# First stage of a one-core decoder block: state-space response from short powers, split gate product, and a new order of the batches

## The chip, the cores and the metric

The kernel runs on 1 core of one Trainium2 chip. The metric is the device time of one execution in microseconds (us), as the median of several runs. The core has five engines that each work through an instruction stream of their own: TensorE (PE in the profile, PEld for its weight loads), VectorE (DVE), ScalarE (ACT), GpSimd (POOL) and SyncE (SP, which only issues DMAs here). They are held together by semaphores: an instruction waits until a semaphore has reached a number, and another instruction raises it when it ends.

## The reference

Input x is 8 batches of 512 tokens with 256 channels. Three residual blocks follow each other, each behind a layer norm: a state-space block, a cross attention over 64 context rows, and a mixture of 8 experts with top 2. Only the first is touched. Its convolution is multiplied by 0 and set to 1, so the state input is the same for each token and each batch:

```python
xc = xc * 0 + 1
dBC = xc @ W_x.T                        # the same row for every token
delta = jax.nn.softplus(dlt @ W_dt.T + b_dt)
A = -jnp.exp(A_log)                     # 512 channels x 16 states
# scan over L: h = exp(delta*A)*h + delta*B ; y = sum over states of h*C
y = ys.transpose(1, 0, 2) + D_skip * xc
out = y * jax.nn.silu(z) @ W_out.T      # z: second half of x @ W_in.T
```

So y depends on channel and position alone. It is the running sum over the position of a kernel: for channel c and distance l, the sum over 16 states of coef times exp(rate * l). What differs between batches is z, and then the product of the gated y with W_out.

## The kernel before, in words

The program has two blocks, with a barrier between them. The first holds the state-space stage (lines 178 to 561), and the second the attention, the shared and the routed experts. Only the first block is changed.

The response. With KE = 4 groups of 128 channels and NS = 16 states there are 64 steps. In each step ScalarE computes exp(rate * l) for l = 1 to 511 of one group and state (`pw`, line 500), and VectorE adds it, times its coefficient, to `kern` (line 424). Four scans turn `kern` into `yD` (line 429). The layer norms and the evacuation of z are threaded between these steps: SLOT = 8 steps for each batch.

The gate. For each of the B = 8 batches VectorE computes statistics (line 111, `stats_part`), GpSimd the inverse deviation (120, 122), VectorE and GpSimd normalise two token tiles each (127), TensorE transposes them (274), ScalarE copies them out of PSUM (`hT`, 479), and TensorE multiplies with `win` in fp32 (287: four parts e of 128 channels, two pieces k of the sum each). ScalarE copies parts 0 to 2 into `sz` (484), VectorE part 3 (420). All eight batches of z are held in `sz`. TensorE goes through all eight, with the keys of the attention (304) behind batch 1, then the values with their bias (314, 315), and then goes on to the output products.

The output. After the response is there, for each batch: silu on ScalarE (506), `gate` on VectorE (440: `sz` times `yD`), `high` on ScalarE (512: the product rounded to fp32r in one of two buffers `gh`), the rest `gl` on VectorE (`low`, line 141, called at 453), `out_part` on TensorE (326: 48 fp32r products, lines 135 to 137, into PSUM banks 6 and 7) and `residual` on VectorE (436: adds the two banks to `X`, and frees them for the next batch). VectorE's order is written out by hand (lines 449 to 462): in turn b it does gate(b+1), the low part of b, residual(b-1). `high(b)` waits for the end of out_part(b-2), whose buffer it takes.

GpSimd spreads the keys into `kbd` (555), 16 instructions behind `yD`.

Of the kernel before, what the change touches and what calls it, by code (L numbers as in the profile page):

```python
# [18 lines left out]
def build(nc, d):  # L19
# [6 lines left out]
    ALU = mybir.AluOpType  # L26
# [3 lines left out]
    P = 128  # L30
# [5 lines left out]
    EI, NS = d["A_log"].shape  # L36
# [21 lines left out]
    with ctx:  # L58
# [84 lines left out]
        SLOT = KE * NS // B  # L143
        PWB = 4
# [8 lines left out]
        sz = Place(prior)("sz", [P, B, KE * L])  # L153
# [6 lines left out]
        hT = ab("hT", [P, 2, KD, L])  # L160
        wq, wk, wv, wo = (ab(n, [P, KD, D]) for n in ("wq", "wk", "wv", "wo"))
        bq, bk = ab("bq", [P, KD]), ab("bk", [P, KD])
        bv = ab("bv", [1, D])
# [9 lines left out]

        with ExitStack() as c:
            tmp = Place(ab.at)
            win_at = tmp.at  # L180
            win = tmp("win", [P, KD, EI])
            wout_at = tmp.at
            wout = tmp("wout", [P, KE, D])
            kbd_at = tmp.at
            wx = tmp("wx", [P, KE, R + 2 * NS])
            wdt = tmp("wdt", [R, EI])
            bdt = tmp("bdt", [P, KE])
            dsk = tmp("dsk", [P, KE])
            alog = tmp("alog", [P, KE, NS])
            steps = tmp("steps", [P, L - 1])  # L190
            onesrow = tmp("onesrow", [P, L])
            dlt = tmp("dlt", [R, 1])
            bc = tmp("bc", [P, 2 * NS])
            dl = tmp("dl", [P, 8, KE])
            rate = tmp("rate", [P, KE, NS])
            coef = tmp("coef", [P, KE, NS])
            pw = tmp("pw", [P, PWB, L - 1])
            kern = tmp("kern", [P, KE, L])
            kbd = Place(kbd_at)("kbd", [P, B, KD, HG * S])

            gh = [Place(hT_at)("gh0", [P, KE * L], F32R), Place(kbd_at + 4 * B * KD * HH * S)("gh1", [P, KE * L], F32R)]
            gl = Place(prior)("gl", [P, B, KE * L], F32R)
            wouts = (Place(win_at)("wouth", [P, KE, D], F32R), Place(wout_at)("woutl", [P, KE, D], F32R))
            x_in = phase_sems(c, " ".join("x_in_%d" % b for b in range(B)))
            hn_ready = phase_sems(c, "hn_ready_by_dve hn_ready_by_pool")
            z_copied = phase_sems(c, "z_copied_by_act z_copied_by_dve")
            (consts_in, w_in, win_in, kv_in, late_in, small_mm, dve_done, act_done, pw_ready, pw_used, s_chain,
             hn_var, hn_rstd, hT_psum, hT_ready, z_psum, sz_ready, w_split, g_high, g_low, yD_ready, g_ready, o_psum,
             x1_ready, k_psum, kT_ready, v_psum, v_ready, vz, k_ready) = phase_sems(c, """consts_in w_in win_in kv_in
                late_in small_mm dve_done act_done pw_ready pw_used s_chain hn_var hn_rstd hT_psum hT_ready  # L210
                z_psum sz_ready w_split g_high g_low yD_ready g_ready o_psum x1_ready k_psum kT_ready v_psum
                v_ready vz k_ready""")
            W_IN, KV_IN, LATE_IN = 16 * 6, 16 * 8, 16 * 7
            with nc.Block() as block:
                @block.sync
                def _(sp):
# [4 lines left out]
                    for dst, src in ((wx[:], d["W_xT"].rearrange("(k p) r -> p k r", p=P)),  # L221
                                     (wdt[:], d["W_dtT"]), (bdt[:], d["b_dt"]), (dsk[:], d["D_skip"]),
                                     (alog[:], d["A_log"].rearrange("(k p) n -> p k n", p=P)),
                                     (steps[:], d["steps"])):
                        sp.dma_start(dst, src).then_inc(w_in, 16)
                    x_load(0)
                    for dst, src in ((ident[:], d["ident"]), (small[:], d["small"])):
                        sp.dma_start(dst, src).then_inc(consts_in, 16)
                    sp.dma_start(win[:], d["W_inT"].rearrange("(k p) e -> p k e", p=P)).then_inc(win_in, 16)
# [9 lines left out]
                    sp.dma_start(bv[:], d["bv"]).then_inc(kv_in, 16)  # L239
                    for b in range(3, B):  # L240
                        x_load(b)
                    sp.dma_start(wout[:], d["W_outT"].rearrange("(k p) e -> p k e", p=P)).then_inc(late_in, 16)
                    for w, n in ((wq, "Wq"), (wo, "Wo")):
                        sp.dma_start(w[:], d[n].rearrange("(k p) e -> p k e", p=P)).then_inc(late_in, 16)
                    for dst, src in ((tri[:], d["tri"]), (causal[:], d["causal"]), (bq[:], d["bq"]),
                                     (bo[:], d["bo"].to_broadcast([P, D]))):
                        sp.dma_start(dst, src).then_inc(late_in, 16)
# [3 lines left out]
                def _(pe):  # L251
                    pe.wait_ge(w_in, W_IN)
                    pe.wait_ge(dve_done, 1)
                    for k in range(KE):
                        nc.tensor.matmul(PS[0:R, 0, 0:1], wx[:, k, 0:R], ones[:, 0:1],
                                         start=k == 0, stop=k == KE - 1)
                    for k in range(KE):
                        last = nc.tensor.matmul(PS[:, 1, 0:2 * NS], ones[:, :], wx[:, k, R:R + 2 * NS],
                                                start=k == 0, stop=k == KE - 1)
                    last.then_inc(small_mm, 1)  # L260
                    pe.wait_ge(dve_done, 2)
                    for k in range(KE):
                        last = nc.tensor.matmul(PS[:, 2, k:k + 1], wdt[:, k * P:(k + 1) * P], dlt[:],
                                                start=True, stop=True)
                    last.then_inc(small_mm, 1)

                    def transposes(b):
                        for half in hn_ready:
                            pe.wait_ge(half, b + 1)
                        if b:  # L270
                            pe.wait_ge(hT_ready, KD * b)
# [6 lines left out]
                    def z_part(b):  # L278
                        pe.wait_ge(hT_ready, KD * b + KD)
                        for e in range(KE):  # L280
                            if b:
                                if e < KE - 1:
                                    pe.wait_ge(z_copied[0], (KE - 1) * (b - 1) + e + 1)
                                else:
                                    pe.wait_ge(z_copied[1], b)
# [5 lines left out]
                    pe.wait_ge(consts_in, 32)  # L291
                    transposes(0)
                    pe.wait_ge(win_in, 16)
                    pe.wait_ge(dve_done, 3)
                    transposes(1)
                    for b in range(B):
                        z_part(b)
                        if b < B - 2:
                            transposes(b + 2)
                        if b == 1:  # L300
                            pe.wait_ge(kv_in, KV_IN)
                            for m in range(KD):
                                for k in range(KD):
                                    last = nc.tensor.matmul(PS[:, 6 + m, :], wk[:, k, m * P:(m + 1) * P],
                                                            ctx2[:, k, :, 0, :], start=k == 0, stop=k == KD - 1)
                                last.then_inc(k_psum, 1)
                    for b in range(B):
                        if b < 6:
                            pe.wait_ge(z_copied[0], (KE - 1) * (B - 1) + b // 2 + 1)
                        else:  # L310
                            pe.wait_ge(z_copied[1], B)
                        vs = PS[:, b // 2, (b % 2) * D:(b % 2 + 1) * D]
                        for k in range(KD):
                            nc.tensor.matmul(vs, ctx2[:, k, b, :, :], wv[:, k, :], start=k == 0, stop=False)
                        nc.tensor.matmul(vs, ones[0:1, :], bv[:], start=False, stop=True).then_inc(v_psum, 1)
                    pe.wait_ge(w_split, 2)
                    pe.wait_ge(kT_ready, KD)

                    def out_part(b):
                        pe.wait_ge(g_low, b + 1)  # L320
                        for t in range(TB):
                            if t % 2 == 0:
                                pe.wait_ge(x1_ready, 2 * b + t // 2 + 1)
                            for e in range(KE):
                                at = e * L + t * P
                                last = product(PS[:, 6 + t // 2, (t % 2) * D:(t % 2 + 1) * D],
                                               (gh[b % 2][:, at:at + P], gl[:, b, at:at + P]),
                                               [w[:, e, :] for w in wouts], e == 0, e == KE - 1)
                            if t % 2:
                                last.then_inc(o_psum, 1)  # L330
                    for b in range(B):
                        out_part(b)

                @block.vector
                def _(dve):
                    n = [0]
# [1441 lines left out]
```

## Time and profile before

| | us |
|---|---|
| median of 3 runs | 993.62 (992.84 to 995.99) |
| profiled execution, its own time | 989.96 |
| span of the trace | 988.3 |
| first block, by the start of the second block's work | 166.4 |
| PE busy, whole span | 923.4 (93%) |
| DVE busy | 625.2 (63%) |
| ACT busy | 556.4 (56%) |
| POOL busy | 347.0 (35%) |

The span is the time from the first to the last instruction; 1.7 us of the profiled execution lie outside it. The busy shares are those of the whole, in which the experts hold most of the time; the changed block is a sixth of it and has to be read by itself. A row of the timeline gives start, length, engine, line, operation, the tiles, the count of merged instructions, and in brackets the idle time before it with what ended it. An fp32 matmul stands in the trace as two instructions, an fp32r one as one. The printed length of a matmul holds its way through the array, so the pace is the distance from start to start.

### The profile page before, as it was taken

What the parts mean: (1) busy time and instruction counts of PE and PEld (TensorE: products, weight loads), DVE (VectorE), ACT (ScalarE), POOL (GpSimd) and SP (SyncE); (2) the same over time, 40 slices, a digit from 0 to 9 for tenths busy, and PEclk for the clock granted to TensorE, in tenths of its full rate; (3) what the DMA queues carried; (4) which work ended last, traced back from release to release, by engine and by line L of the source; (5) the groups of instructions that cost most, each with busy time, mean ns of one, the idle gap of its engine ahead of it and who ended that gap; (6) DMA issues with size and microseconds to landing.
All of it is one profiled execution on the core that took longest, in us unless ns stands there. A gap on an engine that the chain in (4) does not pass through costs nothing.

```text
span 988.3 us, 20180 instructions
## 1 busy us (share of the span) xinstructions
PE 923.4 (93%) x6832; PEld 792.9 (80%) x6833; DVE 625.2 (63%) x1485; ACT 556.4 (56%) x1109; POOL 347.0 (35%) x323
## 2 busy tenths in 40 slices
PE   2998898799999889999999999999999999999996
PEld 2444697455666468888888889999999999999996
DVE  4898897566775666666665566546565646565453
ACT  3688842365545454444644467557565657565552
POOL 3652723222120235555555322424233332423222
PEclk9999999999999999999999999999999999999998
DMA  9200002000000201111112843534325252523222
GB/s 254 92 1 1 1 1 72 21 1 1 1 1 1 94 1 67 68 67 67 68 67 76 264 116 94 134 49 107 66 44 131 42 140 44 130 42 54 44 44 33
DMA packets 49312, 64.21 MB, mean 65 GB/s; under 512 B 10289, under 2 KB 42290, under 8 KB 49138
## 3 DMA queue, kind: packets, MB, share of 16 engines
q0 software_dynamic: 17504, 34.87, 15.2%
q1 hardware_dynamic: 31618, 27.68, 9.6%
q10 hardware_dynamic: 144, 1.05, 0.4%
q8 instruction: 28, 0.46, 0.2%
q14 instruction: 18, 0.15, 0.1%
HBM read 38.82 MB, written 24.77 MB: 64 GB/s over the span
## 4 chain that ended last, share of the span: by engine, by line
PE 71%; DVE 7%; ACT 3%; issue 1%; DMA 0%; POOL 0%; SPq 0%; DVEq 0%; POOLq 0%; ACTq 0%
PE PS L135 20%; PE PS L136 19%; PE PS L137 19%; PE PS L646 3%; DVE mxpad L897 2%; PE PS L1559 2%; PE PS L687 2%; PE PS L673 2%; PE PS L693 1%; ACT recs L802 1%; ACT prT L783 1%; PE PS L1109 1%; DVE mxT L908 1%; DMA xr<-routed_rows 0%; DVE hidl L141 0%
## 5 line engine op out<-in xcount | busy, mean ns | idle before, releaser
L1605 ACT ACTIVATE hideh<-PS,be 128x256 fp32r<-128x256 f32 x280 | 140.5, 502 | 152.4 <-PE PS L137 152.4
L1633 POOL DMA_INDIRECT out_rows<-y,toki x70 | 122.3, 1747 | 268.3 <-DVE y L1673 259.1
L141 DVE TENSOR_TENSOR hidel<-act32e,hideh 128x256 fp32r<-128x256 f32 x280 | 118.4, 425 | 107.9 <-ACT act32e L1607 107.6
L135 PE MATMUL PS<-xTeh,wfch 128*128 128x256 f32 x560 | 159.4, 285 | 2.2 <-issue 1.1
L136 PE MATMUL PS<-xTel,wfch 128*128 128x256 f32 x560 | 158.5, 283 | 0.0
L137 PE MATMUL PS<-xTeh,wfcl 128*128 128x256 f32 x560 | 158.4, 283 | 0.0
L135 PE MATMUL PS<-wprh,hideh 128*128 128x256 f32 x560 | 157.9, 282 | 0.0
L137 PE MATMUL PS<-wprh,hidel 128*128 128x256 f32 x560 | 154.8, 277 | 0.0
L136 PE MATMUL PS<-wprl,hideh 128*128 128x256 f32 x560 | 154.8, 277 | 0.0
L1607 ACT ACTIVATE act32e<-PS,be 128x256 f32<-128x256 f32 x280 | 140.9, 503 | 2.8 <-DVE hidel L141 2.8
L135 PEld LDWEIGHTS PS<-xTeh,wfch 128*128 128x128 f32 x560 | 107.3, 192 | 3.8 <-issue 2.3
L137 PEld LDWEIGHTS PS<-xTeh,wfcl 128*128 128x128 f32 x560 | 107.5, 192 | 0.0
L136 PEld LDWEIGHTS PS<-xTel,wfch 128*128 128x128 f32 x560 | 107.3, 192 | 0.0
L136 PEld LDWEIGHTS PS<-wprl,hideh 128*128 128x128 f32 x560 | 105.3, 188 | 0.0
L135 PEld LDWEIGHTS PS<-wprh,hideh 128*128 128x128 f32 x560 | 105.2, 188 | 0.0
L137 PEld LDWEIGHTS PS<-wprh,hidel 128*128 128x128 f32 x560 | 105.2, 188 | 0.0
L1218 ACT ACTIVATE hidh<-PS,bfs 128x512 fp32r<-128x512 f32 x64 | 44.2, 690 | 57.8 <-PE PS L137 54.2
L120 POOL TENSOR_TENSOR vare<-mv,small 128x4 f32<-128x4 f32 x24 | 9.0, 376 | 189.4 <-DVE mv L115 189.2
L1291 POOL DMA_INDIRECT routed_rows<-rows,slotc x64 | 65.5, 1024 | 24.9 <-issue 19.3
L135 PE MATMUL PS<-wpsh,hidh 128*128 128x256 f32 x256 | 73.5, 287 | 0.3 <-DVE hidl L141 0.3
L137 PE MATMUL PS<-wpsh,hidl 128*128 128x256 f32 x256 | 72.1, 282 | 0.0
L136 PE MATMUL PS<-wpsl,hidh 128*128 128x256 f32 x256 | 72.1, 282 | 0.0
(254 smaller groups left out, 2165.3 us busy)
## 6 DMA issues: line engine op xcount, KB each, us to landing
xr<-routed_rows SPq DMA_DIRECT2D x36, 272.0 KB, 2.8
fcraw<-in_Wfc POOLq DMA_DIRECT2D x8, 1024.0 KB, 6.0
prraw<-in_Wproj POOLq DMA_DIRECT2D x8, 1024.0 KB, 8.6
X<-in_x SPq DMA_DIRECT2D x8, 512.0 KB, 6.1
out_rows<-X SPq DMA_DIRECT2D x8, 512.0 KB, 3.0
routed_rows<-pads SPq DMA_DIRECT2D x8, 272.0 KB, 4.5
out_rows<-y,toki POOLq DMA_INDIRECT x70, 3.8
ctx<-in_ctxT SPq DMA_DIRECT2D x4, 256.0 KB
```

Source lines behind the costliest of these rows:

```text
L135: nc.tensor.matmul(out, wh, xh, start=first, stop=False)
L136: nc.tensor.matmul(out, wh, xl, start=False, stop=False)
L137: return nc.tensor.matmul(out, wl, xh, start=False, stop=last)
L141: return eng.tensor_tensor(out, whole, high.bitcast(F32), ALU.subtract)
L646: last = nc.tensor.matmul(at, qT[rows, b % 2, m, t * P:(t + 1) * P], kbd[rows, b, m, :].rearrange("p (i n) -> p i n", i=2), start=m == 0, ...
L673: nc.tensor.matmul(PS[:, j, :], kbd[rows, b, m, j % 2 * P:(j % 2 + 1) * P], qT[rows, b % 2, m, :], start=True, stop=False, skip_group_chec ...
L687: last = nc.tensor.matmul(PS[32 * j:32 * j + 32, 2, :], onesbd[:, m, :], prT[:, m, j, :], start=m == 0, stop=m == KD - 1, skip_group_check ...
L1218: nc.scalar.activation(hid[0][:, j, :], PS[:, j % 4, :], ACT.Gelu_apprx_tanh, bias=bfs[:, j:j + 1])
L1291: nc.gpsimd.indirect_dma_start(out=RG, out_offset=bass.IndirectOffsetOnAxis(ap=slotc[:, t, m:m + 1], axis=0), in_=rows[:, t, :], in_offset ...
L1605: nc.scalar.activation(hid[0][:, j, :], PS[:, j % 4, 0:BLK], ACT.Gelu_apprx_tanh, bias=bias)
L1607: nc.scalar.activation(act32[:, j % 2, :], PS[:, j % 4, 0:BLK], ACT.Gelu_apprx_tanh, bias=bias).then_inc(h_ready, 1)
L1633: nc.gpsimd.indirect_dma_start(out=out, out_offset=bass.IndirectOffsetOnAxis(ap=toki[:, h:h + 1], axis=0), in_=y[:, h, :], in_offset=None, ...
```

## The change

The response is built in another way. The kernel of distance l is written with l = 64 a + r: powers for r = 0 to 63 and for the eight 64 a, 72 in all, are computed for each channel and state, with 8 channels times 16 states on the 128 partitions and G = 64 such groups. VectorE forms the arguments (4 instructions of 128 x 1152), ScalarE takes their exp (4), VectorE multiplies the 8 long powers with a masked coefficient into `cU` (4 of 128 x 1024). TensorE sums over the states with 64 fp32 matmuls of 64 stationary and 64 moving columns (`kernel_sums`), VectorE copies the result out of PSUM (`kernel_rows`, two), TensorE turns it (32 small transposes, `kernel_turn`), and four scans read it from PSUM. The 64 exps, the 64 accumulations and the 255 KB table of steps are gone.

The gate product is made with high and low parts in fp32r (three matmuls for one), so `win` and the transposed activations are split too: `hTh` by ScalarE, `hTl` by VectorE. ScalarE now evacuates all four parts of z, from batch 2 on with silu in the same instruction. `sz` and `gl` have five slots in place of eight.

The order of the batches is new. z of batches 0 to 3 is made ahead of the response and the values; then TensorE goes, for each b, out_part(b), transposes(b+5), z_part(b+4). VectorE and ScalarE have hand-written orders that go with it. The bias of the values is taken out of the values and multiplied with `wo` into `bo` at the end of the block. GpSimd normalises one tile in batches 0 to 4 (VectorE three), and spreads the keys between its later batches. x of batch 0 is loaded first.

The core of the diff:

```diff
                     def z_part(b, parts=range(KE)):
...
+                            if b == 3 and e >= KD:
+                                pe.wait_ge(yD_ready, 2)
+                            if b == 4:
+                                pe.wait_ge(v_ready, 4 * (e + 1))
                             for k in range(KD):
-                                last = nc.tensor.matmul(PS[:, e, :], win[:, k, e * P:(e + 1) * P],
-                                                        hT[:, b % 2, k, :], start=k == 0, stop=k == KD - 1)
+                                last = product(PS[:, e, :], [w[:, k, e * P:(e + 1) * P] for w in winp],
+                                               [x[:, b % 2, k, :] for x in (hTh, hTl)], k == 0, k == KD - 1)
                             last.then_inc(z_psum, 1)
...
+                    def kernel_sums(half):
...
+                        for q in range(GH // 2):
+                            for j in range(2):
+                                g = GH * j + GH // 2 * half + q
+                                last = nc.tensor.matmul(PS[NB * j:NB * (j + 1), 6 + q // 8, q % 8 * NB:(q % 8 + 1) * NB],
+                                                        powers[:, g, 0:NB], cU[:, g, :], start=True, stop=True,
+                                                        skip_group_check=True)
+                        last.then_inc(raw_psum, 1)
...
                     def out_part(b):
...
-                            if t % 2 == 0:
-                                pe.wait_ge(x1_ready, 2 * b + t // 2 + 1)
+                            if b and t % 2 == 0:
+                                pe.wait_ge(x1_ready, 2 * (b - 1) + t // 2 + 1)
...
+                    transposes(0)
+                    pe.wait_ge(win_split, 2)
+                    z_part(0, range(KE - 1))
+                    transposes(1)
+                    z_part(0, range(KE - 1, KE))
...
+                    transposes(2)
+                    z_part(1)
+                    kernel_sums(0)
+                    transposes(3)
+                    z_part(2)
+                    kernel_sums(1)
+                    keys()
+                    kernel_turn(0)
+                    kernel_turn(1)
+                    transposes(4)
+                    z_part(3)
+                    values()
                     for b in range(B):
                         out_part(b)
+                        if b + 5 < B:
+                            transposes(b + 5)
+                        if b + 4 < B:
+                            z_part(b + 4)
...
                 @block.vector
...
                     gate(0)
+                    stats_part(5)
...
+                    x_low(4)
+                    gate(1)
+                    gate_low(0)
+                    gate(2)
                     for b in range(B):
-                        if b < B - 1:
-                            gate(b + 1)
-                        dve.wait_ge(g_high, b + 1)
-                        low(nc.vector, gl[:, b, :], sz[:, b, :], gh[b % 2][:]).then_inc(g_low, 1)
+                        if b + 5 < B:
+                            apply_part(b + 5)
+                        if b + 1 < B:
+                            gate_low(b + 1)
+                        if b + 3 < B:
+                            gate(b + 3)
+                        if b + 6 < B:
+                            stats_part(b + 6)
+                        if b == 4:
+                            dve.wait_ge(late_in, LATE_IN)
+                            nc.vector.tensor_copy(causal16[:], causal[:])
+                            nc.vector.tensor_copy(ident16[:], ident[:])
+                            nc.vector.tensor_copy(bv[:], bvc[:].unsqueeze(2).to_broadcast([P, KD, P])).then_inc(bv_ready, 1)
...
                         if b:
                             residual(b - 1)
...
+                        if b + 5 < B:
+                            x_low(b + 5)
...
                 @block.scalar
...
-                    for b in range(1, B):
-                        if b < B - 1:
-                            silu(b + 1)
-                        high(b)
+                    for b in range(B):
+                        if b + 1 < B:
+                            high(b + 1)
+                        if b + 5 < B:
+                            evac(b + 5)
+                        if b + 4 < B:
+                            for e in range(KE):
+                                z_evac(b + 4, e)
```

`high(b)` still waits for the end of out_part(b-2).

## Rows read from the trace of the kernel before

**Rows 1.** Windows of the two blocks: busy us, instructions in brackets, granted clock

```profile
core 0: us, PE busy (x) PEld busy (x) DVE busy (x) ACT busy (x) POOL busy (x), PEclk, DMA share, GB/s
0.00:166.40 166.40, 138.18 (x657) 96.60 (x658) 133.00 (x237) 101.07 (x146) 70.74 (x61) 0.97 0.18 52
166.40:988.30 821.90, 785.21 (x6176) 696.31 (x6176) 492.17 (x1248) 455.37 (x964) 276.22 (x262) 0.99 0.27 68
```

**Rows 2.** Timeline, PE: gate products, transposes, keys, values

```profile
36.96 7.03 PE L287 MATMUL PS<-hT,win 128*128 128x512 f32 x16
43.83 1.04 PE L274 MATMUL PS<-ident,hn 128*128 128x128 f32 x8
44.70 3.60 PE L304 MATMUL PS<-ctx,wk 128*128 128x512 f32 x8
...
97.58 1.03 PE L314 MATMUL PS<-wv,ctx 128*128 128x256 f32 x4
```

**Rows 3.** Timeline, PE: output batches, start of the first and border to the second

```profile
112.49 0.55 PE L135 MATMUL PS<-wouth,gh 128*128 128x256 f32 x1 [1.46 <-DVE gl L141]
...
119.39 0.28 PE L136 MATMUL PS<-woutl,gh 128*128 128x256 f32 x1
119.50 0.28 PE L137 MATMUL PS<-wouth,gl 128*128 128x256 f32 x1
122.21 0.42 PE L135 MATMUL PS<-wouth,gh 128*128 128x256 f32 x1 [2.43 <-DVE X L436]
```

**Rows 4.** Timeline, DVE: output batches, and the end of the block

```profile
118.77 2.70 DVE L141 TENSOR_TENSOR gl<-sz,gh 128x2048 fp32r<-128x2048 f32 x1
121.39 1.27 DVE L436 TENSOR_TENSOR X<-X,PS 128x512 f32<-128x512 f32 x2
...
132.51 2.29 DVE L141 TENSOR_TENSOR gl<-sz,gh 128x2048 fp32r<-128x2048 f32 x1
134.72 1.38 DVE L436 TENSOR_TENSOR X<-X,PS 128x512 f32<-128x512 f32 x2
136.01 2.29 DVE L440 TENSOR_TENSOR sz<-sz,yD 128x2048 f32<-128x2048 f32 x1
...
165.00 0.69 DVE L436 TENSOR_TENSOR X<-X,PS 128x512 f32<-128x512 f32 x1 [2.17 <-PE PS L137]
```

**Rows 5.** Timeline, ACT: evacuation, high part, copies of the values

```profile
43.37 0.59 ACT L484 ACTIVATE sz<-PS 128x512 f32<-128x512 f32 x1
...
107.86 1.91 ACT L512 ACTIVATE gh<-sz 128x2048 fp32r<-128x2048 f32 x1 [4.01 <-DVE sz L440]
109.68 4.71 ACT L527 ACTIVATE vbd<-PS 64x128 f32<-64x128 f32 x16
```

**Rows 6.** Groups by shape, 0 to 180 us: busy us, mean ns

```profile
L424 DVE SCALAR_TENSOR_TENSOR kern<-pw,coef,kern 128x511 f32<-128x511 f32 x64 | 45.2, 754 | 5.2 <-ACT pw L500 5.1
...
L555 POOL TENSOR_TENSOR kbd<-kT,small 128x256 f32<-128x256 f32 x16 | 25.2, 1611 | 23.1 <-DVE yD L429 23.1
...
L429 DVE TENSOR_TENSOR_SCAN yD<-onesrow,dsk,kern 128x512 f32<-128x512 f32 x4 | 4.8, 1264 | 0.0
```

**Rows 7.** Timeline, PE: the first small matmuls

```profile
6.54 1.01 PE L255 MATMUL PS<-ones,wx 128*64 128x1 f32 x8 [6.54 <-DMA steps<-in_steps]
7.48 1.91 PE L258 MATMUL PS<-wx,ones 128*128 128x32 f32 x8
```

**Rows 8.** Timeline, PE: fp32r products of 512 columns in the attention

```profile
229.01 0.39 PE L135 MATMUL PS<-hTbh,wqh 128*128 128x512 f32 x1
229.24 0.39 PE L136 MATMUL PS<-hTbl,wqh 128*128 128x512 f32 x1
```

**Rows 9.** Window of 3 us behind a PE pause, columns as above

```profile
122.00:125.00 3.00, 2.79 (x14) 2.82 (x15) 3.00 (x3) 1.59 (x1) 3.00 (x3) 0.56 0.02 5
```

**Rows 10.** Timeline, DVE: norm statistics of one batch

```profile
43.80 1.39 DVE L111 BATCH_NORM_STATS2 stats<-X 128x6 f32<-128x256 f32 x4
45.34 0.38 DVE L115 BATCH_NORM_AGGREGATE mv<-stats 128x2 f32<-128x6 f32 x4
```

More of the change, by code:

```diff
@@ L292, in _ @@
[L292 to L306, printed above, removed]
@@ new lines, in kernel_turn @@
+                    def kernel_turn(half):
+                        pe.wait_ge(ksb_ready, half + 1)
+                        bank = (2, 6)[half]
+                        if half:
+                            pe.wait_ge(ksb_ready, 2)
+                        else:
+                            pe.wait_ge(z_copied, KE * 3)
+                        for a in range(NA):
+                            for j in range(2):
+                                rows = slice(NB * j, NB * (j + 1))
+                                last = nc.tensor.transpose(PS[:, bank + j, a * NB:(a + 1) * NB], ksb[rows, half, a, :],
+                                                           ident[rows, rows])
+                        last.then_inc(kern_psum, 1)
@@ new lines, in keys @@
+                    def keys():
+                        pe.wait_ge(kv_in, KV_IN)
+                        for m in range(KD):
+                            pe.wait_ge(z_copied, KE * 2 + m + 1)
+                            for k in range(KD):
+                                last = nc.tensor.matmul(PS[:, m, :], wk[:, k, m * P:(m + 1) * P],
+                                                        ctx2[:, k, :, 0, :], start=k == 0, stop=k == KD - 1)
+                            last.then_inc(k_psum, 1)
@@ new lines, in values @@
+                    def values():
+                        for b in range(B):
+                            if b % 2 == 0:
+                                pe.wait_ge(z_copied, KE * 3 + b // 2 + 1)
+                            for k in range(KD):
+                                last = nc.tensor.matmul(PS[:, b // 2, (b % 2) * D:(b % 2 + 1) * D], ctx2[:, k, b, :, :],
+                                                        wv[:, k, :], start=k == 0, stop=k == KD - 1)
+                            last.then_inc(v_psum, 1)
@@ new lines, in _ @@
+                    apply_part(0)
+                    t_, na, ex, u, ln, delta, tp, um = (dl[:, i, :] for i in range(8))
+                    dve.wait_ge(small_mm, 2)
+                    link(nc.vector.tensor_tensor(t_, PS[0:G, 6, 8:8 + NE], bdt[:], ALU.add))
+                    link(nc.vector.tensor_scalar(na, t_, -1.0, None, ALU.mult))
+                    nc.vector.tensor_tensor(na, na, t_, ALU.min).then_inc(t_ready, 1)
+                    link(nc.vector.tensor_scalar(tp, t_, 0.0, None, ALU.max))
@@ new lines, in _ @@
+                    dve.wait_ge(win_split, 1)
+                    low(nc.vector, winp[1][:], win[:], winp[0][:]).then_inc(win_split, 1)
+                    dve.wait_ge(t_exp, 1)
+                    nc.vector.tensor_scalar(u, ex, 1.0, None, ALU.add).then_inc(u_ready, 1)
+                    x_low(0)
+                    stats_part(1)
+                    dve.wait_ge(u_ln, 1)
+                    link(nc.vector.tensor_tensor(ln, ln, ex, ALU.mult))
+                    link(nc.vector.tensor_scalar(um, u, -1.0, 1e-30, ALU.add, ALU.max))
@@ new lines, in _ @@
+                    columns(0)
+                    columns(1)
+                    arguments(2)
+                    arguments(3)
+                    x_low(2)
+                    stats_part(3)
+                    columns(2)
+                    columns(3)
+                    apply_part(3)
+                    kernel_rows(0)
+                    stats_part(4)
+                    x_low(3)
+                    apply_part(4)
+                    kernel_rows(1)
+                    dve.wait_ge(kv_in, KV_IN)
@@ new lines, in _ @@
+                    dve.wait_ge(wout_split, 1)
+                    low(nc.vector, wouts[1][:], wout[:], wouts[0][:]).then_inc(wout_split, 1)
+                    x_low(4)
+                    gate(1)
+                    gate_low(0)
+                    gate(2)
+                    for b in range(B):
+                        if b + 5 < B:
[11 more added lines that the diff above has]
+                            nc.vector.tensor_copy(bv[:], bvc[:].unsqueeze(2).to_broadcast([P, KD, P])).then_inc(bv_ready, 1)
+                        if b == B - 1:
+                            dve.wait_ge(x1_ready, 2)
+                            for half in hn_ready:
+                                dve.wait_ge(half, B)
+                            norm_stats(link, tiles(0)).then_inc(hn_var, 1)
```

465 lines of the change are left out of this document (254 added, 211 removed).

## The prediction

> **What bounds the kernel now.** I read the windows of the two blocks first. PE is busy for 785 of the 822 us of the second block and for 138 of the 166 us of the first [rows 1]. The change touches the first block alone, so the whole effect has to be found in those 166 us; what follows the barrier I take as unchanged. The timeline of PE then shows two halves. Up to the values PE works through z with pauses at the start alone: 7.0 us for a batch, 1.04 us for the transposes of one, 3.6 us for the keys, about 1.0 us for the values of a batch [rows 2]. The output products start at 112.49, and the last residual ends at 165.7 [rows 3, 4]. In between lie eight batches of 48 fp32r products at a pace of 0.12 us, 5.7 us each; 46 of the 53 us.
>
> The row to look at longest is the border between the first two output batches. The first ends at 119.6; the second starts at 122.21, and the idle time before it was ended by VectorE's line 436, the residual that frees bank 6 [rows 3]. That bank could have been read long before. VectorE came to it late because it does its work in the order in which it is written: the low part of the next batch stood first, from 118.77 to 121.39, and the residual came behind it [rows 4]. So the residual is on PE's path through what stands ahead of it on VectorE. In later batches of before, the low part ends while PE is still at its products, and the residuals follow in time. The new order has to be read for this.
>
> **What goes.** 64 accumulations of 754 ns on VectorE [rows 6] and 64 exps on ScalarE go. They lay beside z on PE, and since PE ran on through z they are worth little by themselves; they are worth the start of the output, which waited for the response and the low part [rows 3]. z falls from 7.03 us to 24 products of 0.23 us, the pace of the attention's split products of the same shape [rows 2, 8]: 5.5 us a batch, 12 us in all, on PE.
>
> **What comes, up to the first output batch.** Loads: x of batch 0 now goes ahead of the six small loads. Before, PE started when the last of them landed, at 6.54 [rows 7]; I add 1.5 us for the issues ahead of it. Small matmuls 2.9 us [rows 7], a copy, then twice as many of the second kind (eight for four), the first transposes, ScalarE's and VectorE's split of `win` (about 1 us each) and of the first activations: z of batch 0 starts at about 18. From there PE has z for four batches 22.1, four sets of transposes 4.2, keys 3.6, values 8.0 [rows 2]. The kernel sums are 64 fp32 matmuls, 128 trace instructions of 64 by 64 columns, which nothing in before shows. Nearest is the first small matmul at the lower clock level: 0.12 us with 64 stationary columns, 0.24 with 128 [rows 7]. At the upper level that gives 0.06 to 0.12 us each, 7.7 to 15.4 us; I take 0.09, 11.5 us, the middle, since shape speaks for the lower and the fp32 moving pass for the upper one. The 32 turns at 0.1 us make 3.2. Sum 52.6.
>
> The Trainium skill, in "TensorE: Matmul & The Clock Gate", Part 2, says that the time of a weight load grows with the columns loaded. Rows 7 agree, 0.12 us against 0.24. By that rule the sums would cost the lower bound, 7.7 us, and the forecast would be 4 us less.
>
> PE also waits for VectorE here. VectorE has arguments, masks, columns and row copies of 1000 to 1150 elements between the norms; its 2048-element operation takes 2.2 us from start to start [rows 4], so these take 1.2 us each. Walking both orders by these prices, PE waits 1.6 us for the transposes of batch 1, 4.2 for those of batch 2 (low part of batch 1, two arguments, three tiles of normalising stand ahead), 1.3 for those of batch 3. With 3 us for the lower clock at the start and behind the 4 us wait, out_part(0) starts at 18 + 52.6 + 7.1 + 3 = 81. The four scans, the first two gates and low part 0 fit beside z of batch 3 and the values. That is 31 us earlier than 112.49, with z of four batches and three sets of transposes still to do.
>
> **From the first output batch on.** Work of PE: eight times 5.7, four z of 5.5 and three transposes of 1.04, 71 us. If PE never waited, the block would end at 81 + 71 + 2 = 154. It will wait, by the written orders. Before out_part(b), PE needs residual(b-1). On VectorE this stands behind gate_low(b+1), gate(b+3), and for b = 1 the statistics of batch 7. gate_low(b+1) needs high(b+1). On ScalarE high(b+1) stands behind the four evacuations of z of batch b+3. And that z is made by PE after out_part(b-1). So z, evacuation, high part, low part, gate and residual form one chain, and PE sits idle from the end of z(b+3) to the residual. In before high and low part of the next batch depended on an output batch that was one further back, and z was done.
>
> The price of the idle time: last evacuation 0.6, high part 1.9 [rows 5], low part 2.2, gate 2.2, half of the residual 0.7 [rows 4], and four passages between engines of 0.1 to 0.2 us, 0.7 together. Some overlap of start-up brings this to 8.1 us. For b = 2 and 3 that is the wait. For b = 1 the statistics add 1.4 + 0.4 [rows 10]: 9.9. For b = 4 three copies add 1.0: 9.1. For b = 5 and 6 no z and no gate are left, but high(b+1) waits for the end of out_part(b-1), whose buffer it takes: 0.2 + 1.9 + 0.2 + 2.2 + 0.7 + 0.1 = 5.3 each. For b = 7 none. Sum: 9.9 + 8.1 + 8.1 + 9.1 + 5.3 + 5.3 = 45.8 us.
>
> Behind the pause of 2.4 us before 122.21 the granted clock of the next 3 us was 0.56 [rows 9], about its lower level of 1.2 GHz, and the first 14 products took 0.20 us each instead of 0.12: 1.1 us in that window, about 1.5 until it was up. Six pauses longer than this one make 9 us. GpSimd's 16 key spreads of 1.6 us [rows 6] move from beside the first output batches to beside turns 0 to 2. While they ran, the low part took 2.70 us, later 2.29 [rows 4]; about three such operations on the chain, 1.3 us. The tail is longer: bias times `wo` after the last output batch and its addition, 1.6 us against 0.9.
>
> **Sum.** 81 + 71.0 + 45.8 + 9 + 1.3 + 1.6 = 209.7, against 165.7: 44 us slower. On the profiled execution's 989.96 us that is 1034; that execution lies 3.7 us below the median of the three, and on the median it is 1038. Unknown: the sums (4 less, 4 more), VectorE's broadcast operations (4 less to 8 more), the start of z (2 either way), hops and pauses (6 either way), the clock (4 less, 5 more). Taken together 16 either way: 1022 to 1054.
>
> **Rivals.** *The chain doesn't form* (the faster side): gates and low parts come early enough and PE runs through. It decides at the point where z(b+3), evacuation and high part end before out_part(b-1) does. Then the block ends near 154 and 2 us for single waits more, 10 less than 165.7: 984. For it speaks that VectorE's work of a turn, about 10 us, is less than PE's 12.3. Against it stand the order in the code and the 2.43 us row, which is the same mechanism on one link [rows 3]. 6%.
>
> *The front is dear*: kernel sums at the 0.24 us of 128 columns [rows 7] are 31 us instead of 11.5, and VectorE's broadcast operations twice 1.2 us, in part under it. Start of the output some 22 us later: 1060. For it: no such shape in before. Against: rows 7's 64-column figure already is at the lower clock. 8%.
>
> *The clock stays low*: with 8 us pauses in a period of 21 us TensorE would hold its lower level through each burst. A turn's 12.3 us of work would take some 10 more than forecast, four times, and the three later batches 4 each: 1090. Against: behind the single pause of before it was back within 4 us. 4%.
>
> The Trainium skill describes bursts of matmuls with idle stretches between ("TensorE: Matmul & The Clock Gate", HAM oscillation): each burst starts at the lower level and the loss is half of the throttled time. That is a rule against this change, and the trace has it once [rows 9]. By it each of the six pauses costs as one does here, which is the forecast, and the last rival doesn't happen.
>
> *The change does something else to the second block*: the gate is rounded in another way, and a token that goes to another expert could add or take a block of routed work. 2%.
>
> **How the numbers follow.** Forecast 80%, faster rival 6%, dear front 8%, low clock 4%, other 2%. The range of the forecast's own bounds holds its 80%. What a measurement can tell from no change is about 0.3%, 3 us. Faster by over that 6%, within it 1%, slower by over that 93%.
>
> **What would show it.** In the profile after: z of batch 0 from 18; out_part(0) from about 81; then a PE pause of 8 to 10 us before out_part(1) to (4), ended by the residual's line on VectorE, which itself is preceded by low part and gate; ScalarE's high part right behind the fourth evacuation; pauses of 5 us before batches 5 and 6; a granted clock near 0.6 just behind each. If those pauses are ended by something else, or are under 2 us, the prediction is wrong. If PE reaches out_part(0) after 95, the front was misjudged.

## The result, and the profile after

The changed kernel takes 1037.42 us (median of 4 runs, 1035.97 to 1039.1), the kernel before 994.25 (4 runs, 992.84 to 995.99). The ratio is 1.0434, with a 95% interval of 1.0409 to 1.0458: 43 us slower, where 44 were forecast, and inside the range.

The profiled execution took 1037.99 us. The page of after:

```profile
span 1036.1 us, 20463 instructions
...
PE 930.4 (90%) x7046; PEld 825.3 (80%) x7055; DVE 599.3 (58%) x1441; ACT 518.0 (50%) x1052; POOL 327.8 (32%) x318
...
PE   6695774868999988999999989999999999999996
...
PEclk9897787789999999999999999999999999999998
```

VectorE, ScalarE and GpSimd have less to do than before, PE hardly more. Still the span is 48 us longer. The slices show where: in the first eight, some 207 us, PE is at 4 to 9 tenths and its granted clock at 7 to 9. The second block starts at 210.3 in place of 166.4 [rows 1], and that is 44.0 us of it. The other 3.9 lie in the second block, 825.8 us against 821.9, where nothing was changed. That is the spread of single executions: in the profiles of the nine kernels changed here the same second block took 820.4 to 825.8 us. Also, the profiled execution of before lies 4.3 us under its median and the one of after at its median; in the medians the whole difference is 43.2.

The timeline of PE in after, at the first product of each output batch (columns as in rows 2 and 3):

```profile
76.99 0.36 PE L135 MATMUL PS<-wouth,gh 128*128 128x256 f32 x1 [1.93 <-DVE gl L141]
...
101.38 0.55 PE L135 MATMUL PS<-wouth,gh 128*128 128x256 f32 x1 [9.52 <-DVE X L464]
...
122.85 0.55 PE L135 MATMUL PS<-wouth,gh 128*128 128x256 f32 x1 [7.70 <-DVE X L464]
...
145.41 0.55 PE L135 MATMUL PS<-wouth,gh 128*128 128x256 f32 x1 [7.70 <-DVE X L464]
...
166.85 0.55 PE L135 MATMUL PS<-wouth,gh 128*128 128x256 f32 x1 [8.37 <-DVE X L464]
...
180.58 0.55 PE L135 MATMUL PS<-wouth,gh 128*128 128x256 f32 x1 [5.07 <-DVE X L464]
...
194.25 0.55 PE L135 MATMUL PS<-wouth,gh 128*128 128x256 f32 x1 [5.08 <-DVE X L464]
```

These rows answer to rows 3. The output starts 35.5 us earlier than the 112.49 of before. But then PE waits six times for the residual (line 464 now), 43.4 us in all. What the residual waited for is seen on ScalarE and VectorE ahead of 122.85:

```profile
115.19 0.60 ACT L604 ACTIVATE sz<-PS 128x512 f32<-128x512 f32 x1 [0.78 <-PE PS L137]
115.68 1.90 ACT L620 ACTIVATE gh<-sz 128x2048 fp32r<-128x2048 f32 x1
...
117.61 2.29 DVE L141 TENSOR_TENSOR gl<-sz,gh 128x2048 fp32r<-128x2048 f32 x1 [5.17 <-ACT gh L620]
119.82 2.29 DVE L471 TENSOR_TENSOR sz<-sz,yD 128x2048 f32<-128x2048 f32 x1
122.03 1.28 DVE L464 TENSOR_TENSOR X<-X,PS 128x512 f32<-128x512 f32 x2
```

Last evacuation, high part, low part, gate, residual, without a gap between them: the chain of the prediction, from the end of z at 115.15 to the product at 122.85. The profile names only its last link.

### The profile page after: what moved, and what is told of

The parts are those of the page before. It is cut to its first block, busy times and chain, and to the rows that moved or that the text cites. A ratio compares the mean times of both kernels' runs of the same rounds, so it can differ in the third digit from the quotient of the medians.

```text
span 1036.1 us, 20463 instructions
## 1 busy us (share of the span) xinstructions
PE 930.4 (90%) x7046; PEld 825.3 (80%) x7055; DVE 599.3 (58%) x1441; ACT 518.0 (50%) x1052; POOL 327.8 (32%) x318
## 4 chain that ended last, share of the span: by engine, by line
PE 68%; DVE 6%; ACT 2%; issue 1%; DMA 1%; POOL 0%; SPq 0%; DVEq 0%; POOLq 0%; ACTq 0%
PE PS L135 19%; PE PS L136 19%; PE PS L137 19%; PE PS L793 3%; DVE mxpad L1044 2%; PE PS L1706 2%; PE PS L834 1%; PE PS L820 1%; PE PS L840 1%; ACT recs L949 1%; DMA xr<-routed_rows 1%; ACT prT L930 1%; PE PS L1256 1%; DVE hidl L141 1%; DVE mxT L1055 0%
## 5 line engine op out<-in xcount | busy, mean ns | idle before, releaser
L120 POOL TENSOR_TENSOR vare<-mv,small 128x4 f32<-128x4 f32 x24 | 6.7, 281 | 270.4 <-DVE mv L115 270.3
L135 PE MATMUL PS<-wouth,gh 128*128 128x256 f32 x128 | 44.0, 344 | 45.4 <-DVE X L464 43.4
```

Source lines behind the costliest of these rows:

```text
L135: nc.tensor.matmul(out, wh, xh, start=first, stop=False)
```

## The experiments

Where a kernel differs in one place from the changed one, its time is compared with 1.0434 times the kernel before on the same chip: 1035.1 us for the first four kernels (before 992.03), 1034.3 for the others (before 991.27). The times expected for the first five start from the changed kernel's 1037.4 instead, so they are 2 to 3 us high from the outset.

**The residual first.** In VectorE's loop (`+` is the experiment, `-` the changed kernel, here and below):

```diff
                     for b in range(B):
+                        if b:
+                            residual(b - 1)
                         if b + 5 < B:
                             apply_part(b + 5)
...
-                        if b:
-                            residual(b - 1)
                         if b + 5 < B:
                             x_low(b + 5)
```

> The changed kernel, but in each turn b of VectorE's loop residual(b-1) stands first, ahead of the normalising, the low part and the gate. Nothing else differs. Theory (order): the 43.4 us of PE pauses before output batches 1 to 6 (9.5, 7.7, 7.7, 8.4, 5.1, 5.1) come from the residual standing behind low part and gate, whose input is the z made after the previous output batch. Then all six pauses shrink to under 1 us, the lower clock behind them goes too, and the first block ends near 210 - 43 - 12 = 155: about 982 to 987 us, faster than the kernel before the change. Rival (load): a turn is bound by the sum of VectorE's work or by z's three products, whatever the order; then pauses move to another wait (low part, transposes) and the time stays above 1020.

Measured: 979.77 us, 0.9871 of before (0.9841 to 0.9902). 55 us less than the changed kernel, and 12 less than before. This is 2 us under the range expected: the first block ends at 156.2, 1 us later than reckoned, and the second block took 822.3 us in this profile, not the 825.8 of after. One pause is left, before output batch 5:

```profile
135.44 0.35 PE L135 MATMUL PS<-wouth,gh 128*128 128x256 f32 x1 [2.69 <-DVE X L464]
```

On VectorE, residual 4 stood there behind low part 5, gate 7 and the three copies, the last of which began at 134.41. The rival, a turn bound by its load, is out: the work of a turn is the same, only its order changed.

**The high part early.** In ScalarE's loop:

```diff
+                    high(1)
                     for b in range(B):
-                        if b + 1 < B:
-                            high(b + 1)
+                        if b + 2 < B:
+                            high(b + 2)
                         if b + 5 < B:
                             evac(b + 5)
```

> The changed kernel, but ScalarE makes high(b+2) at the beginning of turn b, ahead of the evacuations of batches b+5 and b+4, as soon as out_part(b) has ended. VectorE's order stays. Theory (order): high part 1.9 and low part 2.2 leave the chain and lie beside transposes and z; left are last evacuation, gate and residual. The pauses before output batches 1 to 4 fall from 9.5, 7.7, 7.7, 8.4 to about 5.6, 3.8, 3.8, 4.5; those before 5 and 6 stay at 5.1. That is 15.6 us less: about 1021. Rival (load): under 5 us less.

Measured: 1016.89 us, 1.0251 of before (1.0209 to 1.0293), 18 less than the changed kernel. Pauses of 5.58, 4.48, 3.70, 4.37, 5.08 and 5.07 us, against 5.6, 3.8, 3.8, 4.5, 5.1, 5.1 expected; the first block is 14.9 us shorter. The one pause that is longer than expected, 4.48 before output batch 2, has low part and gate at 2.70 us each in place of 2.29, while GpSimd spread keys beside them:

```profile
111.86 2.70 DVE L141 TENSOR_TENSOR gl<-sz,gh 128x2048 fp32r<-128x2048 f32 x1
114.48 2.70 DVE L471 TENSOR_TENSOR sz<-sz,yD 128x2048 f32<-128x2048 f32 x1
```

The last evacuation began at 113.48 and took 0.60, so here the low part, and not the evacuation, was the last thing ahead of the gate.

**The residual ahead of the gate.** The two lines of `residual` stand directly behind `gate_low(b + 1)`, and no longer at the end of the turn:

```diff
                         if b + 1 < B:
                             gate_low(b + 1)
+                        if b:
+                            residual(b - 1)
                         if b + 3 < B:
                             gate(b + 3)
```

> The changed kernel, but residual(b-1) stands behind the low part and ahead of gate(b+3), the statistics and the three copies. Theory (order): only what is taken out of the chain comes off, 2.2 + 1.8 at batch 1, 2.2 at 2 and 3, 2.2 + 0.9 at 4, nothing at 5 and 6: pauses of 5.5, 5.5, 5.5, 5.3, 5.1, 5.1, 11.5 us less, about 1026. Rival (load): under 4 us less, since VectorE has the same work in each turn.

Measured: 1021.73 us, 1.0303 of before (1.0266 to 1.0339), 13 less. The pauses:

```profile
96.93 0.55 PE L135 MATMUL PS<-wouth,gh 128*128 128x256 f32 x1 [5.50 <-DVE X L464]
...
116.47 0.55 PE L135 MATMUL PS<-wouth,gh 128*128 128x256 f32 x1 [5.50 <-DVE X L464]
...
168.10 0.55 PE L135 MATMUL PS<-wouth,gh 128*128 128x256 f32 x1 [5.07 <-DVE X L464]
```

5.50 four times, 5.07 and 5.08. What is taken out of the chain comes off the pause and nothing else does. In this and the last experiment the median fell 2 to 3 us more than the pauses did, which is within the intervals. In the profiles the first block fell by 13.5 us here, with 11.3 off the pauses, and by 14.9 there, with 15.2 off them; so the lower clock behind the pauses didn't cost the same in each of these executions.

**The pauses filled.** PE multiplies into a free bank before it waits:

```diff
                     for b in range(B):
+                        if 0 < b < B - 1:
+                            pe.wait_ge(hT_low, KD * min(b + 5, B))
+                            for i in range((0, 38, 30, 30, 34, 19, 19)[b]):
+                                nc.tensor.matmul(PS[:, 4, :], winp[0][:, 0, 0:P], winp[1][:, 0, :],
+                                                 start=True, stop=True)
                         out_part(b)
```

> The changed kernel, but PE issues matmuls into a free bank, whose result nobody reads, in the pauses before output batches 1 to 6 (38, 30, 30, 34, 19, 19 of 0.22 us each), so that it is busy while it waits. The chain that ends the wait is the same. If the lower clock behind the pauses costs what the trace shows by the lengths of the output batches (7.2 us for batch 1 and 8.3 to 8.5 for batches 2 to 6 in place of 5.7), the time falls by 1.5 + 5 x 2.7 = 15 us less what the filling adds, to 1023 to 1027. If the clock isn't what makes these batches long, nothing changes: 1037.

Measured: 1020.42 us, 1.028 of before (1.0251 to 1.0309), 15 less than the changed kernel, though PE has 170 matmuls more. The windows of 3 us at the start of output batches 1, 2 and behind the latter, in after (busy us by engine, then the granted clock as the fraction before the last two numbers):

```profile
101.40:104.40 3.00, 3.00 (x14) 3.00 (x15) 0.43 (x1) 0.00 (x0) 0.86 (x1) 0.50 0.02 5
122.80:125.80 3.00, 2.95 (x14) 2.98 (x15) 0.50 (x1) 0.00 (x0) 0.00 (x0) 0.50 0.00 0
125.80:128.80 3.00, 3.00 (x17) 3.00 (x17) 0.00 (x0) 0.00 (x0) 0.00 (x0) 0.55 0.00 0
```

and at the start of output batches 1 and 2 in the kernel with filled pauses:

```profile
103.30:106.30 3.00, 3.00 (x25) 3.00 (x26) 0.41 (x1) 0.00 (x0) 0.83 (x1) 1.00 0.00 0
123.30:126.30 3.00, 2.98 (x25) 3.00 (x26) 0.47 (x1) 0.00 (x0) 0.00 (x0) 1.00 0.00 0
```

14 products in 3 us at a granted clock of 0.50 (1.2 GHz), 25 at 1.00 (2.4 GHz). What is left of the six waits, 0.64 to 0.87 us each, is ended by the same line as before, the residual. The first block is 11.6 us shorter in the profile and the whole 15 in the medians. In the profile output batch 1 starts 1.9 us later than in after (103.26, not 101.38), for a reason ahead of the first filling: z of batch 4 began at the lower clock behind a wait of 2.4 us. From there to the end of the block the filled kernel is 13.5 us shorter. So of the 55 us between the changed kernel and the residual-first one, 12 to 15 were the lower clock after the pauses, and the rest the pauses.

**z in fp32 again.** One part undone, `low(...)` in `x_low` being a plain copy:

```diff
-                                last = product(PS[:, e, :], [w[:, k, e * P:(e + 1) * P] for w in winp],
-                                               [x[:, b % 2, k, :] for x in (hTh, hTl)], k == 0, k == KD - 1)
+                                last = nc.tensor.matmul(PS[:, e, :], win[:, k, e * P:(e + 1) * P],
+                                                        hTl[:, b % 2, k, :], start=k == 0, stop=k == KD - 1)
```

> The changed kernel with one part undone: z is one fp32 matmul again in place of three fp32r ones; VectorE copies the whole transposed activations where it took the low part. Orders, kernel sums and all else stay. A batch of z takes 7.0 us on PE in place of 5.5. If the split is worth what PE saves where PE or the chain behind z is late: batches 4 to 7 stand on the chain, 4 x 1.5 = 6 us; of batches 0 to 3 the first two run into PE's waits of 4.2 and 4.7 us for VectorE and cost nothing, the others 3: 9 us slower than the changed kernel, about 1046. If z isn't on the path at all: the same as the changed kernel within 3 us.

Measured: 1042.46 us, 1.0525 of before (1.0504 to 1.0546), 8 us slower than the changed kernel, where 9 were expected. Output batch 0 starts at 79.40 in place of 76.99, and the pauses are the same (9.52, 7.70, 7.70, 8.38, 5.08, 5.07).

**z in fp32 with the residual first.** The edits of the first experiment and of the last one together.

> The same undoing in the kernel with the residual first. There PE is busy through nearly all of the part with output batches, so each of the four later z costs its 1.5 us, and the two ahead of the values too: 9 us slower than the kernel with the residual first, about 989, still a few us faster than before. If the gain of the residual-first kernel over the kernel before came from the split alone, this one would be no faster than before.

Measured: 987.16 us, 0.9969 of before (0.9953 to 0.9985), 7 to 10 slower than the kernel with the residual first (7.4 by the medians, which are from two chips, 7.7 by the first block of the profiles, 10 by the ratios). The split product is worth some 8 us in either order. By the ratios the residual-first kernel is 13 us faster than before; 10 of them, three quarters, are the split, and 3 us, of which the interval leaves 1.5 to 4.7, stay without it. So the order repairs the loss, and most of what is gained beyond that comes from the split product.

**Both orders.** The edits of the first two experiments together.

> The kernel with the residual first, and with high(b+2) at the beginning of ScalarE's turn b, as in the second experiment. The residual-first kernel has one pause of 2.7 us left, before output batch 5, ended by residual 4, which stands behind low part 5, gate 7 and three copies. With the high part early this goes: 3 us less, 1 of it the clock, about 977. If the pauses that were left came from something else: no difference.

Measured: 975.2 us, 0.9845 of before (0.9823 to 0.9867). No pause of over 1 us is left on PE behind output batch 0; the first block ends at 150.7. By the ratios that is 3 us less than with the residual alone, as expected, though it is near the intervals' width; in the profiles the first block is 5.5 us shorter, 1.0 of it ahead of output batch 0, where nothing differs.

**The front too.** The kernel with both orders, and this:

```diff
-        BY_DVE = [3] * 5 + [2] * (B - 5)
+        BY_DVE = [3] * 6 + [2] * (B - 6)
...
+                    apply_part(2)
                     arguments(0)
                     arguments(1)
-                    apply_part(2)
...
+                    x_low(2)
+                    stats_part(3)
                     arguments(2)
                     arguments(3)
-                    x_low(2)
-                    stats_part(3)
+                    apply_part(3)
                     columns(2)
                     columns(3)
-                    apply_part(3)
```

> As the last one, and the order of VectorE ahead of the first output batch: apply of batch 2 ahead of arguments 0 and 1; low part and statistics of batch 2 and 3 ahead of arguments 2 and 3, and apply of batch 3 ahead of columns 2 and 3; three tiles of batch 5 on VectorE in place of two, since GpSimd took 12.4 us for its two beside the gates. PE's waits before the transposes of batches 2 and 3, 4.4 and 5.4 us, fall to about 2 each, with 1 to 2 us of lower clock: 6 to 8 us less than the last one, about 970. If the front isn't on the path (values or response late for another reason): within 2 us of the last one.

Measured: 971.1 us, 0.9798 of before (0.9775 to 0.982): the fastest of all, 20 us under the kernel before. It gave 4 to 5 us of the 6 to 8 expected. PE in this kernel, before the transposes of batches 2 and 3 and output batch 0:

```profile
27.45 1.79 PE L275 MATMUL PS<-ident,hn 128*128 128x128 f32 x8 [1.92 <-DVE hn L127]
...
41.45 1.94 PE L275 MATMUL PS<-ident,hn 128*128 128x128 f32 x8 [3.78 <-DVE hn L127]
...
71.74 0.36 PE L135 MATMUL PS<-wouth,gh 128*128 128x256 f32 x1 [1.93 <-DVE gl L141]
```

The first wait fell from 4.2 to 1.9, the second only to 3.8, and the one for low part 0 stayed. Output batch 0 starts 4.0 us earlier than with both orders alone. The tile of batch 5 that went from GpSimd to VectorE gave the remaining 1.0: from output batch 0 to the transposes of batch 5 it is 7.3 us, not 8.3.

## Why the prediction was right, step by step

**The chain.** Right in its place, its links and its size. Pauses forecast: 9.9, 8.1, 8.1, 9.1, 5.3, 5.3, none; measured 9.52, 7.70, 7.70, 8.37, 5.07, 5.08, none. The sum of 45.8 was 43.4. The second and third experiments each take other links out, and each pause falls by those links to within 0.2 us, but for the one of 4.48 us beside GpSimd's spreads. The first experiment takes the residual out of the chain, and five of six pauses go.

**The start of the output.** Forecast 81, measured 77.0. z of batch 0 started at 17.0 (forecast 18). Two terms of the front were mis-sized, the kernel sums and the clock. The sums:

```profile
39.88 2.09 PE L302 MATMUL PS<-cU,powers 128*64 128x64 f32 x64
...
54.76 2.09 PE L302 MATMUL PS<-cU,powers 128*64 128x64 f32 x64
60.41 1.21 PE L317 MATMUL PS<-ident,ksb 64*128 64x64 f32 x32
```

Two halves of 2.1 us, a pace of 0.033 us, where the bounds were 0.06 to 0.12: 4.2 us in place of 11.5, and 1.2 in place of 3.2 for the turns. The measured sum lies outside the bounds, below the lower.
Sums and turns saved 9.3 us, the start, the values and the transposes some 3 more, and two thirds of it were given back. PE waited 4.7 us for the transposes of batch 3, not 1.3, since VectorE was no earlier, and 1.9 for low part 0, where I had none; the 1.6 for those of batch 1 never came. And the lower clock ahead of the output cost about 7.4 us, not 3: 2.7 at the first z, 2.9 in transposes and z behind the wait of 4.2 us, 1.8 behind the wait of 4.7 (each against 0.23 us a product and 0.8 a set of transposes).

The broadcast operations cost 1.3 and 1.2 us, about as worked out:

```profile
L433 DVE TENSOR_TENSOR powers<-rcT,steps 128x1152 f32<-128x1152 f32 x4 | 5.2, 1352 | 0.0
L441 DVE TENSOR_TENSOR cU<-cmask,powers 128x1024 f32<-128x1024 f32 x4 | 4.8, 1216 | 2.4 <-ACT powers L613 2.4
```

**The clock.** Under-sized: 9 us forecast, about 14 read behind the six pauses. From one pause of 2.4 us I took 1.5 us of loss for all. Batch 1 took 7.2 us from its first product to the next transposes (101.38 to 108.62), which is that figure; batch 2 took 8.3 (122.85 to 131.15), batch 3 7.4 (145.41 to 152.79), batches 4, 5 and 6 8.4 to 8.5 (166.85 to 175.3, 180.58 to 189.0, 194.25 to 202.7), against 5.7 at full clock. So the loss behind one pause is 1.5 to 2.8 us, and the one pause that I had to go by was at the low end. The filled pauses confirm the size. It also came behind the 1.9 us pause before output batch 0, which I hadn't counted: 7.4 us in place of 5.7. That one cost nothing in the end. Where the same batch ran at full clock, as in the kernels with the early high part and with the filled pauses, PE waited 2.4 us for the transposes of batch 5 in place of 0.9, and they began 8.3 us after output batch 0 all the same.

**GpSimd.** Wrong in kind and small in size. I expected 1.3 us, since its key spreads would slow VectorE on the chain. They took 612 ns each in after, not 1611 [rows 6], in VectorE's idle time, and the low parts took 2290 ns in the mean, their undisturbed value. In the residual-first kernel, where the pauses are gone, two such operations of the loop take 2.58 and 2.70 us again.

**Sum.** 77.0 + 71 + 43.4 + 0.9 (a wait for the transposes of batch 5) + 16 + 1.6 = 209.9, the forecast's 209.7: the errors, 4 us in the front, 2.4 in the pauses and 1.3 for GpSimd against 7 for the clock and 0.9 for the wait, cancelled. The 4 in the front are themselves 12 too much against 8 too little. That the total came out within 1 us is luck. The closeness of the total says less than the six pauses do.

**A row that I read too strongly.** The pause before 122.21 [rows 3] was given as the residual standing behind a low part. The residual did stand there, but that low part was itself needed by the same output batch, and ended at 121.4. Without the residual behind it the pause would have been some 0.7 us shorter, not gone. What carried the forecast was the order in the code. I also wrote that PE had pauses at the start alone up to the values; there is one more, of 2.76 us, ahead of the transposes at 81.26:

```profile
81.26 1.83 PE L274 MATMUL PS<-ident,hn 128*128 128x128 f32 x8 [2.76 <-issue]
```

No term of the sum hangs on it.

**The rivals.** The faster side was said to be decided by whether z, evacuation and high part end before the previous output batch does. With the order of the changed kernel they can't. Its price, 984, was near what the residual-first order then gave, 979.8. The dear front is out, since the output started at 77.0. The lasting low clock is out too: behind each of the six pauses the pace of the full clock came back within the output batch, after 3.3 to 5.8 us. The second block has the same numbers of instructions on VectorE, ScalarE and GpSimd as before (1248, 964, 262), which speaks against the last.

## What to carry to other kernels

When the batches of a loop are moved against each other, write down for each engine what stands ahead of the instruction that frees a buffer, and follow it through the other engines' orders; one cheap operation (here a residual of 0.7 us) behind two or three that look ahead turned what could have been a gain of 12 us, the residual-first kernel's, into a loss of 43. That the first output came 35 us earlier says little by itself, since z of four batches had only been moved behind it. Put what frees a buffer for the engine that bounds the kernel first in its turn, and work for later batches behind it. And price a pause of TensorE with the lower clock that follows it: here a third again of the pause.

## What the runs showed of the hardware that was not expected

GpSimd nearly stops beside VectorE's gates. In after its two tiles of batch 5 took this long, while VectorE went through three gates and two low parts, and the next ones this:

```profile
72.82 12.37 POOL L127 TENSOR_SCALAR hn<-X,mv,rstd 128x256 f32<-128x256 f32 x2 [0.31 <-POOL rstd L122]
85.16 2.33 POOL L687 TENSOR_TENSOR kbd<-kT,small 128x256 f32<-128x256 f32 x4
...
89.16 2.68 POOL L127 TENSOR_SCALAR hn<-X,mv,rstd 128x256 f32<-128x256 f32 x2 [0.31 <-POOL rstd L122]
```

12.4 us against 2.7 for the same work. VectorE's own operations kept their 2.3 us. The same two tiles took 12.37 us in each of the seven other kernels that have them there. It is otherwise beside the key spreads, which have two inputs like VectorE's gates: there both are slower, GpSimd 1.1 to 1.6 us for a spread in place of 0.6, VectorE 2.6 to 2.7 in place of 2.3.

The Trainium skill ("GPSIMD Engine Reference", Specifications) says that GpSimd shares its SBUF interfaces with VectorE, with contention when VectorE's instruction has two SBUF inputs; gate and low part are such instructions, and the trace agrees. It also delays PE's transposes of batch 5. Their row names no releaser (0.85 us of "issue" ahead of 85.28), but GpSimd's tiles end at 85.19, and with one tile fewer on GpSimd, in the last experiment, that wait is gone.

Small fp32 matmuls in a row, with 64 stationary and 64 moving columns, passed at 33 ns per trace instruction, 66 ns for a whole one, when they wrote by turns to two halves of the PSUM partitions; in one half alone none was run.
